# Norm in a four-layer block: per-column statistics once in a 128x512 bank per chunk, and a quarter of the high halves made by ScalarE

## The chip, the cores and the metric

One core of a Trainium2 chip runs the whole kernel. The metric is the device time of one execution in microseconds, as the median of several runs.

## The reference

The input x has 256 x 256 tokens of 64 channels, in fp32. Four layers of the same kind follow each other, each adding to x. Cut to what matters:

```python
xn = layernorm(x, norm_w, norm_b)              # over the 64 channels
left  = (xn @ Wl) * sigmoid(xn @ Wlg)          # some layers times a mask
right = (xn @ Wr) * sigmoid(xn @ Wrg)
og = sigmoid(xn @ Wog)
out = einsum('bikh,bjkh->bijh', left, right)   # or over k and the other side
out = layernorm(out, onorm_w, onorm_b) * og
x = x + out @ Wo
```

The change is in the first line: the normalisation of x in each layer.

## The kernel before, in words

Each layer is one block with a program per engine. The work is staged: `norm`, `project` (first half of the channels), a contraction, `project` (second half), a contraction, `finish`. The first two of them meet at the change: `norm` writes the normalised x to DRAM as two fp16 tensors, a high and a low part (XH or XHA), and `project` loads them again.

`norm` works on 16 chunks of 2048 columns by 128 partitions (two sides of 64 channels), a chunk being two tiles of 128x1024, so there are 32 tiles; tile t belongs to chunk t // 2. Per tile:

- `center` (TensorE, L663): eight 64x64 fp32 matmuls (four matmuls of two passes each) subtract the channel mean and scale by one number for the layer. The output is one of three two-bank PSUM buffers, `banks[t % 3]`. It waits until `scale` of tile t-3 has read that buffer, and for the first tile of a chunk until the chunk was loaded.
- `square` (ScalarE, L686), PSUM to SBUF.
- `vary` (TensorE, L670): two 128x128 matmuls with the constant K_MEAN make the mean of the squares over 64 channels, repeated on all 64 partitions of the side, in `banks[3]`.
- `root` (ScalarE, L692 and L696): logarithm, then exponential of -0.5 times it, both 128x1024.
- `scale` (VectorE, L712): the centred PSUM value plus a bias, times the result, to a ring of four SBUF tiles.
- `halve` (VectorE, L722 and L724): the high half as fp16, then what is left over as the low half. VectorE's order is scale(t), halve(t-1).

TensorE's order is center(0), center(1), and then vary(t), center(t+2) for each t. ScalarE's is square(t+1), root(t).

SyncE issues the transfers (L618, L626, L277, L298). The loads of x go to three chunk buffers; the load of chunk n+3 waits until both tiles of chunk n were centred. Its loop is, for each n:

```python
if n + 3 < from_dram:
    sp.wait_ge(centered.s, centered.n + 2 * n + 2)
    load_xt_chunk(sp, n + 3, n % 3)
if n >= 1:
    store(n - 1, (n - 1) % 2)   # waits for lows_ready of 2n tiles, then 4 DMAs
```

A load moves 1 MB, each of the four stores of a chunk 256 KB. In the first layer only eight chunks are loaded (`from_dram` is 8); the other eight stand in SBUF, and are stored to XT here, one DMA each. In the other layers all 16 are loaded, the first three outside this loop. At the end of the loop SyncE issues the first loads for `project`.

## Time and profile before

| | |
|---|---|
| median of 3 runs | 2152.81 us (2152.39 to 2152.84) |
| the profiled execution, its own time | 2150.95 us |
| its span, first to last instruction | 2148.8 us |
| mean granted TensorE clock | 0.956 |
| TensorE busy | 1888.1 us, 88% |
| VectorE busy | 1693.6 us, 79% |
| ScalarE busy | 1591.5 us, 74% |

The profile is of one execution. Durations in the next sections but one come from it; the time of an execution is 2.15 us more than its span. Busy shares are means over all stages. A line such as L663 is a line of the kernel's file. An instruction's duration contains the latency to its end, so that the next instruction of an engine can begin a little before it ends.

### The profile page before, as it was taken

The page shows a single profiled execution, that of the slowest core. Times are in us where ns is not written, and L with a number is a line of the kernel's source. Part 1 is how long each engine was busy: PE and PEld are TensorE (multiplying, and loading weights), DVE is VectorE, ACT ScalarE, POOL GpSimd, SP SyncE. Part 2 cuts the span into 40 slices and gives each one's busy share as a digit, 9 for nine tenths or more (in the row PEclk, how much of TensorE's full clock was granted, in tenths as well). Part 3 has the DMA queues.
Part 4 walks back from the last instruction along what each step waited for, and adds up shares of the span by engine and source line. Part 5 has one row for each costly group of instructions (what it writes and reads, how often), then busy time and mean ns, then how long its engine had stood idle before and what let it go on. Part 6 is the DMA issues. An engine that isn't in the chain of part 4 may idle for free. (4 is left out here: it accounts for less than half of the span.)

```text
span 2148.8 us, 44715 instructions
## 1 busy us (share of the span) xinstructions
PE 1888.1 (88%) x14485; PEld 1280.8 (60%) x14492; DVE 1693.6 (79%) x2690; ACT 1591.5 (74%) x2204; POOL 595.4 (28%) x574
## 2 busy tenths in 40 slices
PE   5687979699897998989989799899997879899998
PEld 4423959455422786855622697886552258777665
DVE  6798989989598877688969887878776977677665
ACT  3598969679897756569989775766888966566666
POOL 0001918175100000026400470732870000000755
PEclk8899989999999999999999999999999999999999
DMA  9589938279798739169979954917997993753897
GB/s 393 195 274 312 264 79 235 94 290 384 270 302 275 277 117 312 41 245 402 410 261 316 265 145 150 278 43 278 407 393 256 308 303 130 245 186 127 320 350 299
DMA packets 297397, 549.53 MB, mean 256 GB/s; under 512 B 14768, under 2 KB 170416, under 8 KB 273712
## 3 DMA queue, kind: packets, MB, share of 16 engines
q1 hardware_dynamic: 295680, 538.38, 72.9%
q10 hardware_dynamic: 1584, 9.51, 1.1%
q8 instruction: 68, 1.11, 0.2%
q14 instruction: 65, 0.53, 0.1%
HBM read 371.67 MB, written 176.16 MB: 255 GB/s over the span
## 5 line engine op out<-in xcount | busy, mean ns | idle before, releaser
L1603 POOL TENSOR_TENSOR LR<-LR 128x512 f32<-128x512 f32 x128 | 187.9, 1488 | 523.3 <-DVE LR L1649 501.2
L802 PE MATMUL bank<-whigh,kept 128*128 128x128 f16 x2048 | 268.2, 231 | 30.5 <-DMA kept<-XH 22.5
L1594 POOL TENSOR_TENSOR LR<-LR,sum 128x2048 f32<-128x2048 f32 x30 | 136.5, 4549 | 526.4 <-DVE LR L1408 526.4
L802 PEld LDWEIGHTS bank<-whigh,kept 128*128 128x128 f16 x2048 | 261.5, 150 | 34.6 <-issue 26.3
L802 PE MATMUL bank<-wlow,kept 128*128 128x128 f16 x2048 | 267.4, 230 | 0.0
L802 PEld LDWEIGHTS bank<-wlow,kept 128*128 128x128 f16 x2048 | 261.9, 150 | 0.0
L670 PE MATMUL bank<-LR,kst 128*128 128x512 f32 x512 | 254.3, 619 | 8.3 <-ACT LR L692 6.3
L865 POOL TENSOR_TENSOR msgs<-sigs,mask_sb 128x256 f32<-128x256 f32 x192 | 124.6, 663 | 487.1 <-ACT sigs L839 481.9
L1497 PEld LDWEIGHTS bank<-kst,LR 128*128 128x128 f32 x1024 | 151.0, 192 | 109.9 <-issue 90.7
L1509 PE MATMUL bank<-LR,wog 128*128 128x512 f16 x768 | 211.9, 385 | 4.8 <-ACT msgs L1550 4.0
L670 PEld LDWEIGHTS bank<-LR,kst 128*128 128x128 f32 x512 | 87.6, 191 | 179.1 <-issue 172.9
L812 PE MATMUL bank<-whigh,kept 128*128 128x128 f16 x2048 | 153.4, 226 | 37.1 <-DMA kept<-XHA 32.7
L1007 PE MATMUL bank<-LR 128*128 128x256 f32 x768 | 172.7, 387 | 7.0 <-DVE LR L904 4.2
L1263 PE MATMUL bank<-LR 128*128 128x256 f32 x768 | 169.9, 385 | 7.0 <-DVE LR L904 4.2
L1497 PE MATMUL bank<-kst,LR 128*128 128x128 f32 x1024 | 159.3, 279 | 14.7 <-ACT sigs L1545 7.7
L1007 PEld LDWEIGHTS bank<-LR 128*128 128x128 f32 x768 | 148.6, 194 | 28.3 <-DVE LR L904 4.6
L1263 PEld LDWEIGHTS bank<-LR 128*128 128x128 f32 x768 | 148.0, 193 | 28.2 <-DVE LR L904 4.6
L692 ACT ACTIVATE LR<-bank,epsx 128x1024 f32<-128x1024 f32 x128 | 142.9, 1116 | 25.7 <-PE bank L670 21.6
L812 PEld LDWEIGHTS bank<-whigh,kept 128*128 128x128 f16 x2048 | 121.1, 101 | 64.5 <-issue 36.3
L686 ACT ACTIVATE LR<-bank,small 128x1024 f32<-128x1024 f32 x128 | 140.8, 1100 | 16.5 <-PE bank L663 16.5
L839 ACT ACTIVATE sigs<-bank,small 128x256 f32<-128x256 f32 x256 | 121.1, 478 | 31.8 <-PE bank L802 25.4
L696 ACT ACTIVATE LR<-LR 128x1024 f32<-128x1024 f32 x128 | 135.5, 1058 | 4.0
(189 smaller groups left out, 4106.1 us busy)
## 6 DMA issues: line engine op xcount, KB each, us to landing
LR<-XT SPq DMA_DIRECT2D x103, 1024.0 KB, 8.9
kept<-XH SPq DMA_DIRECT2D x128, 512.0 KB, 5.8
kept<-XHA SPq DMA_DIRECT2D x128, 512.0 KB, 5.1
XT<-LR SPq DMA_DIRECT2D x56, 1024.0 KB, 9.0
LR<-XH SPq DMA_DIRECT2D x64, 512.0 KB, 6.7
LR<-XHA SPq DMA_DIRECT2D x64, 512.0 KB, 6.0
OS<-kept SPq DMA_DIRECT2D x12, 2048.0 KB, 7.5
LR<-OS SPq DMA_DIRECT2D x48, 512.0 KB, 8.5
```

Source lines behind the costliest of these rows:

```text
L670: last = pe.matmul(banks[3][:, u * BANK:(u + 1) * BANK], K(K_MEAN), sq[t % 3][:, u * BANK:(u + 1) * BANK], start=True, stop=True)
L686: act.activation(sq[t % 3], banks[t % 3][:, :], ACT.Square, bias=cb).then_inc(squared.s, 1)
L692: act.activation(lnv[t % 2], banks[3][:, :], ACT.Ln, bias=epsx[:, :], scale=1.0 / X_SCALE ** 2).then_inc(logged.s, 1)
L696: act.activation(rs[t % 3], lnv[t % 2], ACT.Exp, scale=-0.5).then_inc(rooted.s, 1)
L802: last = pe.matmul(bank(g)[:, j * P:(j + 1) * P], tokens(h, g // 4, g % 4, j, slice(0, P)), w[:, half * P:(half + 1) * P], start=part == 0 ...
L812: pe.matmul(bank(2 * q + s)[:, j * P:(j + 1) * P], tokens(h, s, q, j, slice(0, P)), whigh[:, half * P:(half + 1) * P], start=j == 0, stop= ...
L1007: last = pe.matmul(banks[e % 3][:, c * N:(c + 1) * N], src[:, kt, off_a + ch, ut * P:(ut + 1) * P], src[:, kt, off_b + ch, :], start=kt == ...
L1263: last = pe.matmul(banks[e % 3][:, c * N:(c + 1) * N], src[:, kt, off_a + 4 * g + c, ut * P:(ut + 1) * P], src[:, kt, off_b + 4 * g + c, : ...
L1497: last = pe.transpose(by_token(turn_bank(t))[:, :, j, :], n_t[c % len(nrm)][:, :, 4 * q + j], K(K_IDENT))
L1509: last = pe.matmul(bank(2 + t % 2), wog[w][:, :], pair_cols(x, q) if k_is_b else by_b(x, q), start=(w, part) == (0, 0), stop=w == 1)
L1594: pool.tensor_tensor(v, v, token(sum2, c, C), ALU.mult).then_inc(normalized.s, 1)
L1603: pool.tensor_tensor(by_b(x_of(c), q) if end else by_token_cols(x_of(c), q), by_token(gated[t % 4]), by_token_cols(xi[c % len(xi)], q), AL ...
```

## The change

The statistics are no longer made for each of the 64 partitions of a side, but once per column. `vary(n)` works on a chunk: four fp32 matmuls with 32 output columns (the constant K_STAT) put the variances of the chunk's four column blocks of 512 into four groups of 32 partitions of one 128x512 bank. There are two such banks in turn. Logarithm and exponential are made once per chunk on that bank. `spread_out(t)` is new: two fp32 matmuls over 32 rows each (K_SPREAD) carry a tile's values to all 128 partitions, into `banks[2]`.

`center` now alternates between `banks[0]` and `banks[1]`, and waits for the square of tile t-2 in place of `scale`. `take_out(t)` is new on ScalarE: it copies the centred tile, with the bias added, to one of six SBUF tiles. `scale` is a plain product of that tile and the spread values. In every fourth tile (3, 7, 11, ...) ScalarE makes the high half (`high_half`), and VectorE waits for it and makes the low half. The orders of TensorE and ScalarE are rewritten; those of VectorE and SyncE stay.

```diff
-K_CENTER, K_MEAN, K_GROUP, K_IDENT, K_DROP, K_LAST, K_SIDE, K_CENTER_OUT, K_END = \
-    0, 128, 256, 384, 512, 640, 768, 770, 898
+K_CENTER, K_SPREAD, K_GROUP, K_IDENT, K_DROP, K_LAST, K_SIDE, K_CENTER_OUT, K_STAT, K_END = \
+    0, 128, 256, 384, 512, 640, 768, 770, 898, 930
...
                          for v in (sum1, sum2))
-            sq, yc, lnv, rs = ([ar.take(GW) for _ in range(k)] for k in (3, 2, 2, 3))
+            sq, yc, xc = ([ar.take(GW) for _ in range(k)] for k in (1, 2, 6))
+            sq += [squares[0][:, :], squares[1][:, :], rings[0][0]]
             yc += [obuf[1][:, i * GW:(i + 1) * GW] for i in range(2)]
+            lnv, deviations = ([v[:, i * BANK:(i + 1) * BANK] for i in range(2)] for v in (ar.take(GW), rings[1][0]))
+            spread_rs, stat_bank = banks[2], [banks[3][:, i * BANK:(i + 1) * BANK] for i in range(2)]
             from_dram = FROM_DRAM if number == 0 else NCH
             cb, k_is_b = small[:, 7:8], layer["k_is_b"]
             per, tiles = 64, 2 * NCH
+            elsewhere = list(range(3, tiles, 4))
+            own = [t for t in range(tiles) if t not in elsewhere]
+
+            def parts_of(t):
+
+                h = t // 2 % 2
+                y, to, rest = (v.rearrange("p (s f) -> p s f", s=2) for v in (yc[t % 4], high[h], low[h]))
+                to, rest = (v[:, :, t % 2 * BANK:(t % 2 + 1) * BANK] for v in (to, rest))
+                return y, to, rest
+
             @block.sync
             def _(sp):
                 def store(n, h):
@@ -649,11 +667,11 @@
                     h = n % 3
                     if u == 0 and n < from_dram:
                         pe.wait_ge(loaded[h].s, loaded[h].n + 16 * (n // 3) + 16)
-                    pe.wait_ge(normed.s, normed.n + t - 2)
+                    pe.wait_ge(squared.s, squared.n + t - 1)
                     for half in range(2):
                         for s in range(2):
                             rows = slice(C * s, C * s + C)
-                            to = banks[t % 3][C * half:C * half + C, s * BANK:(s + 1) * BANK]
+                            to = banks[t % 2][C * half:C * half + C, s * BANK:(s + 1) * BANK]
                             x = xa[h] if n < from_dram else entered(n)
                             if k_is_b:
                                 cols = x[rows, (2 * half + u) * BANK:(2 * half + u + 1) * BANK]
...
@@ -663,64 +681,104 @@
                             last = pe.matmul(to, cen[rows, rows], cols, start=True, stop=True)
                     last.then_inc(centered.s, 1)
 
-                def vary(t):
-                    pe.wait_ge(squared.s, squared.n + t + 1)
-                    pe.wait_ge(logged.s, logged.n + t)
+                def vary(n):
+                    pe.wait_ge(squared.s, squared.n + 2 * n + 2)
+                    pe.wait_ge(logged.s, logged.n + n - 1)
                     for u in range(2):
-                        last = pe.matmul(banks[3][:, u * BANK:(u + 1) * BANK], K(K_MEAN),
-                                         sq[t % 3][:, u * BANK:(u + 1) * BANK], start=True, stop=True)
+                        for s in range(2):
+                            q = 2 * u + s
+                            last = pe.matmul(stat_bank[n % 2][32 * q:32 * q + 32, :], kst[:, K_STAT:K_STAT + 32],
+                                             sq[(2 * n + u) % 4][:, s * BANK:(s + 1) * BANK], start=True, stop=True)
                     last.then_inc(variance.s, 1)
 
-                center(0)
-                center(1)
-                for t in range(tiles):
-                    vary(t)
-                    if t + 2 < tiles:
-                        center(t + 2)
+                def spread_out(t):
+                    n, u = divmod(t, 2)
+                    pe.wait_ge(rooted.s, rooted.n + n + 1)
+                    pe.wait_ge(normed.s, normed.n + t)
+                    for s in range(2):
+                        rows = slice(32 * (2 * u + s), 32 * (2 * u + s) + 32)
+                        last = pe.matmul(spread_rs[:, s * BANK:(s + 1) * BANK], kst[rows, K_SPREAD:K_SPREAD + P],
+                                         deviations[n % 2][rows, :], start=True, stop=True)
+                    last.then_inc(spread.s, 1)
+
+                for t in range(3):
+                    center(t)
+                for n in range(NCH):
+                    vary(n)
+                    if n >= 1:
+                        spread_out(2 * n - 1)
+                    for t in (2 * n + 3, 2 * n + 4):
+                        if t < tiles:
+                            center(t)
+                    spread_out(2 * n)
+                spread_out(tiles - 1)
 
             @block.scalar
             def _(act):
+                def take_out(t):
+                    act.wait_ge(centered.s, centered.n + t + 1)
+                    act.wait_ge(normed.s, normed.n + t - 5)
+                    act.activation(xc[t % 6], banks[t % 2][:, :], ACT.Identity, bias=cb).then_inc(taken_out.s, 1)
+
                 def square(t):
-                    act.wait_ge(centered.s, centered.n + t + 1)
-                    act.wait_ge(variance.s, variance.n + t - 2)
-                    act.activation(sq[t % 3], banks[t % 3][:, :], ACT.Square, bias=cb).then_inc(squared.s, 1)
-
-                def root(t):
-
-                    act.wait_ge(variance.s, variance.n + t + 1)
-                    act.wait_ge(rooted.s, rooted.n + t - 1)
-                    act.activation(lnv[t % 2], banks[3][:, :], ACT.Ln, bias=epsx[:, :],
+                    act.wait_ge(variance.s, variance.n + t // 2 - 1)
+                    act.activation(sq[t % 4], banks[t % 2][:, :], ACT.Square, bias=cb).then_inc(squared.s, 1)
+
+                def logarithm(n):
+                    act.wait_ge(variance.s, variance.n + n + 1)
+                    act.wait_ge(rooted.s, rooted.n + n - 1)
+                    act.activation(lnv[n % 2], stat_bank[n % 2], ACT.Ln, bias=epsx[:, :],
                                    scale=1.0 / X_SCALE ** 2).then_inc(logged.s, 1)
-                    act.wait_ge(logged.s, logged.n + t + 1)
-                    act.wait_ge(normed.s, normed.n + t - 2)
-                    act.activation(rs[t % 3], lnv[t % 2], ACT.Exp, scale=-0.5).then_inc(rooted.s, 1)
-
+
+                def root(n):
+                    act.wait_ge(logged.s, logged.n + n + 1)
+                    act.wait_ge(spread.s, spread.n + 2 * n - 2)
+                    act.activation(deviations[n % 2], lnv[n % 2], ACT.Exp, scale=-0.5).then_inc(rooted.s, 1)
+
+                def high_half(t):
+                    y, to, _ = parts_of(t)
+                    act.wait_ge(normed.s, normed.n + t + 1)
+                    act.wait_ge(stored[t // 2 % 2].s, stored[t // 2 % 2].n + per * (t // 4))
+                    act.activation(to, y, ACT.Identity, bias=scale1[:, :]).then_inc(odd_highs.s, 1)
                 for h in range(4):
                     act.wait_ge(stored[h].s, stored[h].n)
-                square(0)
-                for t in range(tiles):
-                    if t + 1 < tiles:
-                        square(t + 1)
-                    root(t)
+                for t in range(2):
+                    take_out(t)
+                    square(t)
+                for n in range(NCH):
+                    if n + 1 < NCH:
+                        take_out(2 * n + 2)
+                        square(2 * n + 2)
+                    logarithm(n)
+                    if n + 1 < NCH:
+                        take_out(2 * n + 3)
+                    root(n)
+                    if 2 * n - 1 in elsewhere:
+                        high_half(2 * n - 1)
+                    if n + 1 < NCH:
+                        square(2 * n + 3)
+                high_half(tiles - 1)
 
             @block.vector
             def _(dve):
                 def scale(t):
 
-                    dve.wait_ge(rooted.s, rooted.n + t + 1)
+                    dve.wait_ge(spread.s, spread.n + t + 1)
+                    dve.wait_ge(taken_out.s, taken_out.n + t + 1)
                     dve.wait_ge(lows_ready.s, lows_ready.n + t - 3)
-                    dve.scalar_tensor_tensor(yc[t % 4], banks[t % 3][:, :], cb, rs[t % 3], ALU.add, ALU.mult).then_inc(normed.s, 1)
+                    dve.tensor_tensor(yc[t % 4], spread_rs[:, :], xc[t % 6], ALU.mult).then_inc(normed.s, 1)
 
                 def halve(t):
 
-                    h = t // 2 % 2
-                    y, to, rest = (v.rearrange("p (s f) -> p s f", s=2) for v in (yc[t % 4], high[h], low[h]))
-                    to, rest = (v[:, :, t % 2 * BANK:(t % 2 + 1) * BANK] for v in (to, rest))
+                    y, to, rest = parts_of(t)
                     dve.wait_ge(normed.s, normed.n + t + 1)
                     if t % 2 == 0:
-                        dve.wait_ge(stored[h].s, stored[h].n + per * (t // 4))
-                    dve.tensor_scalar(to, y, X_SCALE, None, ALU.add).then_inc(highs_ready.s, 1)
-                    dve.wait_ge(highs_ready.s, highs_ready.n + t + 1)
+                        dve.wait_ge(stored[t // 2 % 2].s, stored[t // 2 % 2].n + per * (t // 4))
+                    if t in elsewhere:
+                        dve.wait_ge(odd_highs.s, odd_highs.n + elsewhere.index(t) + 1)
+                    else:
+                        dve.tensor_scalar(to, y, X_SCALE, None, ALU.add).then_inc(highs_ready.s, 1)
+                        dve.wait_ge(highs_ready.s, highs_ready.n + own.index(t) + 1)
                     dve.scalar_tensor_tensor(rest, y, X_SCALE, to, ALU.add, ALU.subtract).then_inc(lows_ready.s, 1)
 
                 for h in range(4):
...
     k[:, K_CENTER:K_CENTER + P] = np.eye(P) - same_side / C
     k[:, K_CENTER_OUT:K_CENTER_OUT + P] = np.eye(P) - same_side / C
-    k[:, K_MEAN:K_MEAN + P] = same_side / C
+    k[:, K_SPREAD:K_SPREAD + P] = (np.arange(P)[:, None] % 32 == 0) & (np.arange(P)[None, :] < C)
+    k[:, K_SPREAD:K_SPREAD + P] += (np.arange(P)[:, None] % 32 == 16) & (np.arange(P)[None, :] >= C)
```

## Rows read from the trace of the kernel before

**Rows 1.** The page, part 1: busy us (share of the span) and instructions

```profile
PE 1888.1 (88%) x14485; PEld 1280.8 (60%) x14492; DVE 1693.6 (79%) x2690; ACT 1591.5 (74%) x2204; POOL 595.4 (28%) x574
```

**Rows 2.** Stretches: us, busy time of each engine, TensorE clock, DMA share, GB/s

```profile
640.00:650.00 10.00, 9.18 (x40) 2.69 (x36) 9.45 (x10) 9.37 (x10) 0.00 (x0) 1.00 0.93 311
```

**Rows 3.** Timeline, first layer's norm: start, us, engine, line

```profile
139.99 1.28 DVE L712 SCALAR_TENSOR_TENSOR LR<-bank,small,LR 128x1024 f32<-128x1024 f32 x1 [0.28 <-ACT LR L696]
...
141.32 1.09 PE L663 MATMUL bank<-LR,cen 64*64 64x512 f32 x8 [0.36 <-DVE LR L712]
...
142.15 1.06 ACT L696 ACTIVATE LR<-LR 128x1024 f32<-128x1024 f32 x1
...
142.34 1.98 PE L670 MATMUL bank<-LR,kst 128*128 128x512 f32 x4
...
143.11 1.10 ACT L686 ACTIVATE LR<-bank,small 128x1024 f32<-128x1024 f32 x1
...
144.36 1.11 ACT L692 ACTIVATE LR<-bank,epsx 128x1024 f32<-128x1024 f32 x1 [0.15 <-PE bank L670]
...
146.60 1.28 DVE L712 SCALAR_TENSOR_TENSOR kept<-bank,small,LR 128x1024 f32<-128x1024 f32 x1 [0.22 <-ACT LR L696]
...
147.80 0.68 DVE L722 TENSOR_SCALAR sum<-kept 128x1024 f16<-128x1024 f32 x1
```

**Rows 4.** Groups by line and form: busy, mean ns, idle before

```profile
L1641 DVE SCALAR_TENSOR_TENSOR LR<-bank,prm,LR 128x512 f32<-128x512 f32 x128 | 95.1, 744 | 16.7 <-PE bank L1516 15.0 <-DMA LR<-XT 1.1
...
L1634 DVE TENSOR_TENSOR sigs<-bank,msgs 128x512 f32<-128x512 f32 x64 | 43.8, 685 | 1.8 <-issue 1.8
...
L1021 ACT ACTIVATE kept<-bank 128x1024 f32<-128x1024 f32 x48 | 49.2, 1025 | 92.6 <-PE bank L1007 86.9 <-DVE sum L1056 5.7
...
L1381 ACT ACTIVATE sum<-sum,epso 128x256 f32<-128x256 f32 x8 | 4.0, 504 | 1.2 <-DVE sum L1374 1.2
...
L1383 ACT ACTIVATE sum<-sum 128x256 f32<-128x256 f32 x8 | 3.3, 418 | 0.3
```

**Rows 5.** Lines 663 and 812, second layer: ns min/median/max, first and last start

```profile
L663 PE MATMUL bank<-LR,cen x176: 589/611/1112, 571.7 to 676.3; 64*64 64x512 f32 x176
...
L812 PE MATMUL bank<-whigh,kept x62: 219/314/314, 687.0 to 699.9; 128*128 128x128 f16 x62
```

**Rows 6.** Timeline of SyncE's queue and its neighbours, second layer's norm

```profile
602.59 1.23 DVE L724 SCALAR_TENSOR_TENSOR LR<-LR 128x1024 f16<-128x1024 f32 x1
...
603.90 3.41 SPq L277 DMA_DIRECT2D XHA<-LR  x4
...
607.36 1.10 SPq L298 DMA_DIRECT2D LR<-XT  x1
...
618.97 1.09 PE L663 MATMUL bank<-LR,cen 64*64 64x512 f32 x8 [0.46 <-DVE kept L712]
```

**Rows 7.** Loads (L298): load 5, loads 6 to 15; first layer's 3 to 7

```profile
DMA to landing us min/median/max: 7.4/7.4/7.4
...
DMA to landing us min/median/max: 7.3/8.4/8.9
...
DMA to landing us min/median/max: 4.7/7.6/8.7
```

**Rows 8.** Timeline, end of the first layer's norm

```profile
192.81 3.04 SPq L277 DMA_DIRECT2D XH<-sum  x4
...
195.95 2.12 SPq L303 DMA_DIRECT2D kept<-XH  x2
...
202.86 0.33 PE L802 MATMUL bank<-whigh,kept 128*128 128x128 f16 x1 [5.69 <-DMA kept<-XH]
```

**Rows 9.** Waits on TensorE at 1212:1222, and the stretch behind

```profile
PE bank L802 <- DVE LR L893: 2.1, 1, 2.1
...
1215.70:1219.10 3.40, 3.40 (x35) 3.40 (x34) 1.24 (x4) 1.91 (x4) 1.23 (x2) 0.50 1.17 290
```

**Rows 10.** Timeline, the first two tiles' centring in the second layer

```profile
571.75 3.69 PE L663 MATMUL bank<-LR,cen 64*64 64x512 f32 x16 [0.71 <-PEq L545]
```

More of the change, by code:

```diff
@@ L170, in build @@
         epsx = sb("epsx", [P, 1])
+        scale1 = sb("scale1", [P, 1])
         banks = [ctx.enter_context(nc.psum_tensor(f"bank{i}", [P, GW], F32)) for i in range(4)]
@@ L190, in build @@
         centered = sem("centered")
+        taken_out = sem("taken_out")
         variance = sem("variance")
+        spread = sem("spread")
         squared = sem("squared")
@@ L196, in build @@
         highs_ready = sem("highs_ready")
+        odd_highs = sem("odd_highs")
         lows_ready = sem("lows_ready")
@@ L446, in _ @@
                 dve.memset(epsx[:, :], EPS / X_SCALE ** 2)
+                dve.memset(scale1[:, :], X_SCALE)
         fold_project, fold_turn, fold_spread, fold_act, fold_start, fold_copy, fold_greatest, fold_row, fold_rest = fold(0)
@@ L733, in norm @@
             advance(*((loaded[h], 16 * len(range(h, from_dram, 3))) for h in range(3)), (stored[2], 16 * (NCH - from_dram)), (stored[0], per * NCH // 2), (stored[1], per * NCH // 2),
-                    (centered, 2 * NCH), (variance, 2 * NCH), (squared, 2 * NCH), (logged, 2 * NCH),
-                    (rooted, 2 * NCH), (normed, 2 * NCH), (highs_ready, 2 * NCH),
+                    (centered, 2 * NCH), (taken_out, 2 * NCH), (squared, 2 * NCH), (variance, NCH), (logged, NCH),
+                    (rooted, NCH), (spread, 2 * NCH), (normed, 2 * NCH), (highs_ready, len(own)),
+                    (odd_highs, len(elsewhere)),
                     (lows_ready, 2 * NCH))
@@ L1697, in constants @@
     k[:, K_CENTER_OUT:K_CENTER_OUT + P] = np.eye(P) - same_side / C
-    k[:, K_MEAN:K_MEAN + P] = same_side / C
+    k[:, K_SPREAD:K_SPREAD + P] = (np.arange(P)[:, None] % 32 == 0) & (np.arange(P)[None, :] < C)
+    k[:, K_SPREAD:K_SPREAD + P] += (np.arange(P)[:, None] % 32 == 16) & (np.arange(P)[None, :] >= C)
+    k[:, K_STAT:K_STAT + 32] = (np.arange(P)[:, None] // C == np.arange(32)[None, :] // 16) / C
     k[:, K_GROUP:K_GROUP + P] = (pair_of[:, None] == pair_of[None, :]) / 4
```

## The prediction, made before the change was run

> **What bounds the kernel now.** I read the page first: TensorE is busy for 88% of the span, VectorE 79%, ScalarE 74% [rows 1]. That is an average over stages, and the change touches one of them, the norm, which runs four times. So the second view was the table of stretches inside a norm. The reader is to see there that three engines and the DMA engines are all at 92 to 95% [rows 2]. Busy shares don't say which one decides. The timeline does [rows 3]. Follow one tile's chain: `scale` (L712, starts 139.99, 1.28 us) ends; `center` starts 0.05 us behind it (141.32); TensorE, in order, starts `vary` 1.02 us later (142.34, 1.98 us); logarithm 144.36, an exponential of 1.06 behind it, next but one `scale` 146.60 to 147.88. From end of `scale` to end of `scale`: 147.88 - 141.27 = 6.61 us for two tiles, one chunk. It is a loop of latencies, not a full engine: ScalarE's next square starts at 143.11, 0.96 us after an exponential of 1.06 us began (142.15), so instructions that don't wait for each other overlap by 0.10 us, and the pitch of a free 128x1024 one is 1.00 us. A norm takes 687.0 - 571.7 = 115.3 us from its first `center` to the first matmul of `project` [rows 5].
>
> The third view is the DMA queue's own [rows 6, 7]. SyncE issues in program order: the four stores of chunk c-5, then the load of chunk c. In the second layer's norm, `halve` of tile 5 ends at 602.59 + 1.23 = 603.8; the stores are issued from 603.90 for 3.41 us (3.04 in [rows 8], where less else is under way), load 7 at 607.36; loads take 8.4 us to land (7.3 to 8.9), so it is there at about 615.8, and `center` of tile 14, which reads it, starts at 618.97. Slack: 3 us. No wait shows it, and the change spends it.
>
> **The change, part by part.** Hops, all from [rows 3]: 0.05 us into TensorE, 0.04 from it, 0.03 between ScalarE and VectorE. Tiles are numbered from 0, chunk n has tiles 2n and 2n+1, R(n) is the end of `root(n)`.
>
> *ScalarE.* Removed: a 128x1024 logarithm and exponential per tile (1.12 and 1.06 us). Added: one 128x512 pair per chunk, one `take_out` per tile, a `high_half` every fourth tile. `take_out` has the shape and bias operand of the square: 1.10 us; its lower bound is the plain copy of that shape, 1.025 [rows 4]; I take 1.10. Exponential of 512 columns: 256 take 0.418 and 1024 take 1.058, so 0.63. Logarithm: 256 take 0.504, 1024 take 1.116, so 0.70 [rows 3, 4]. `high_half`: 1.06 to 1.10. Sum of pitches per chunk: 4 x 1.00 + 0.60 + 0.53 + 0.50 = 5.6 us, under today's 6.6.
>
> *VectorE.* `scale` becomes a product of a PSUM and an SBUF operand: 0.685 us at 512 columns [rows 4] and the 0.53 us that the next 512 cost in this engine's fp32 forms (1.28 against 0.74) give 1.22 us. A high half takes 0.68, a low half 1.23 [rows 3, 6]. `halve` starts 0.08 before `scale` ends; less such overlaps it is 5.6 us per chunk. Not the bound.
>
> *TensorE.* `center` stays: four quadrants at once, all eight fp32 passes in 1.09 us [rows 3]. The 32-row `spread_out` and 32-column `vary` are not in the trace. If their groups run at once like the quadrants, which differ in rows and in columns, a block takes 1.09 us with the next starting 1.02 later; if one after another, `spread_out` (two matmuls of two passes) takes `vary`'s 1.98 us and the new `vary` (four) about 3.7. I take 1.09, as the quadrants are the nearest row; the other end is a rival. The Trainium skill, TensorEngine Tiling (Array Packing), Tiling Modes, says that a change of tiling mode drains the engine, and the new order changes mode four times per chunk, which speaks against it. The row on `center` then `vary` is such a change and costs 1.02 to the next start: already in my blocks. A full drain, 1.09 each, would add some 2 us to the whole.
>
> *The loop without any transfer.* Chunk with a `high_half` (every other): R, high half (pitch 1.0), square ends R+2.0; `vary` +0.05, `spread_out` +1.02, `center` +1.02, its end +1.13, `take_out` pitch 1.0, `root` 0.63: 6.85 us. Other chunks: `spread_out(2n)` 0.05+1.09, `scale` 0.05+1.22, `spread_out(2n+1)` 0.05+1.02, `center` 1.13, `take_out` 1.0, `root` 0.63: 6.25. Mean 6.55 against 6.61: nothing is won by the halved work, because the chain got two matmul blocks. The head: R(0) about 10.5 us behind the first `center` (1.9 us for each of the first two at the low clock [rows 10]). R(12) = 10.5 + 5 x 6.85 + 7 x 6.27 = 88.6, and `center(30)`, behind square and three blocks, 5.1 later: 93.7. The tail: after `center(30)` come three blocks, `take_out(31)`, `root(14)`, `spread_out(28)`, `scale(28)`, the halves of 27, the stores of chunk 13 (3.1 us) and the first load of `project`, 6.9 us (issue 195.95, first matmul 202.86 [rows 8]): 20.8 us. 114.5 us, against 115.3.
>
> *The loads, where the cost is.* Today `center` of tile 2c waits for `scale(2c-3)`; the low halves that release the stores of chunk c-5 follow `scale(2c-8)`: five tiles between, 15 us. After it, `center(2c)` waits only for squares and for its place behind `spread_out(2c-5)`, which needs `scale(2c-6)`: two tiles. Worked out: halves of 2c-9 end at R+3.6 or R+4.3, `center(2c)` is ready at R+11.3, so 7.0 to 7.7 us are left, and the queue needs 3.1 to 3.4 of issuing and the landing. With idle transfers ahead of the stores, load 5 took 7.4 us behind the first stores (issue 593.74) [rows 7]. 10.5 is over 7.7, for every load from chunk 5 on. Then a new loop closes, two chunks long: load(c) lands, `center(2c)` 0.97 to the next start, `spread_out(2c-4)` queued behind it 1.09, hop and pitch of `scale` 1.18, high half 0.72 (not where ScalarE made it), low half 1.23, SyncE's hop and four issues 3.25, load(c+2) lands 7.3, hop 0.05: 15.8 us (15.1 without the high half; the slower of the two interleaved loops leads). TensorE idles some 3 us in each. A gap of 2.1 us was followed by half clock for 3.4 us elsewhere [rows 9], and a `center` takes 1.85 instead of 1.09 then; as that will not happen each time, I add 0.5: 16.3.
>
> `center(10)` can start when load 5 is there: R(1) is 16.7, the halves of tile 1 end 4.3 later at 21.0, issues 3.1 [rows 8], landing 7.3: 31.5. `center(30)`: 31.5 + 5 x 16.3 = 113.0 instead of 93.7, so 19.3 late, and a norm is 19.3 - 0.8 = 18.5 us longer. Three layers: 55.5. The first layer loads eight chunks only, the rest stands in SBUF, and its loads land up to 8.7 us late [rows 7]: `center(10)` at 32.8, `center(14)` 17.6 later at 50.4, against 10.5 + 3 x 6.27 + 6.85 + 5.1 = 41.3: 9.1, less 0.8: 8.3. Sum: +63.8 us. The profiled execution took 2150.95 us (span 2148.8 and 2.15 around it): 2214.8; the median of the runs stands 1.86 above it: **2216 us**. The constants, the one memset, the new semaphores lie in the first 90 us beside loads: nothing. `project` and later stages move, unchanged.
>
> **The rivals.** *The loads come in time.* For it: 4.7 us is the shortest landing [rows 7]. It decides at 2 x 6.55 - 8.5 = 4.6 us. Against it: that was without stores ahead, and these always stand ahead. Then each norm is 0.8 shorter and the sum is 2150, or about 2136 if `take_out`, blocks and hops are also each at their lower ends (0.25 less per chunk, 56 chunks): the case on the other side.
> *The groups don't run at once.* If `spread_out` takes 1.98, the load loop grows by 0.9: 15 x 0.9 = 14, 2230. If `vary` takes 3.7 too, the chain of the squares is the longer: 6.55 + 2.6 + 0.9, some 3.4 us over today's for 56 chunks, 2340.
> *The clock falls in each idle stretch and stays low for the blocks behind it.* `center` and `spread_out` cost 0.8 each more, 1.6 per loop instead of 0.5: 16 x 1.1 = 18, 2234. For it, the 2.1 us gap; against it, gaps of 0.3 to 0.4 us in every tile cost nothing today [rows 3].
>
> **How the numbers follow.** Forecast 0.74; loads in time 0.13; groups in turn 0.06; low clock 0.07. Around the forecast, landings of 6.5 to 8.5 us (16 loops x 0.8 down, 1.2 up) and issuing of 3.0 to 3.4 give 2200 to 2240. The range 2180 to 2245 adds partly smaller stalls below and the clock above; outside are most of the first rival and a slow `vary`. Within 0.2% (4 us, about what a measurement of this kernel can tell from no change) lies part of the first rival: faster 0.08, same 0.04, slower 0.88.
>
> **What would show it.** `center` (the new line of its matmul) waiting for the DMA of `xt` in every chunk from 5 on, 2 to 4 us; pairs of chunks 16 us apart; loads landing in 7 to 8 us; ScalarE and VectorE waiting for TensorE; DMA share in a norm falling from 0.93 to under 0.8; `take_out` at 1.10, `spread_out` and `vary` blocks at 1.09. A norm of some 134 us where the layer loads all chunks, 124 in the first. I am wrong if `center` never waits for a load, if a load behind four stores lands in under 5 us, or if a later stage takes back the delay.

## The result

The changed kernel took **2268.9 us** (median of 4 runs, 2262.1 to 2274.8), the kernel before, on the same chip, 2152.6 (4 runs): a ratio of 1.054 [1.051, 1.058]. It is slower, by 116 us where 63.8 were forecast. The direction and the place were right, the size was not, and the time lies outside the range (2180 to 2245).

The page of the profile after, against [rows 1]: all three engines are idle for longer, and TensorE's clock is lower.

```profile
span 2269.4 us, 45750 instructions
PE 1948.0 (86%) x15004; PEld 1264.1 (56%) x15004; DVE 1662.8 (73%) x2659; ACT 1553.3 (68%) x2236; POOL 594.5 (26%) x574
PEclk8887989999876899989977699999997769999999
L721 ACT ACTIVATE LR<-bank,small 128x1024 f32<-128x1024 f32 x128 | 142.7, 1115 | 144.5 <-PE bank L681 140.0
L769 DVE TENSOR_TENSOR LR<-bank,LR 128x1024 f32<-128x1024 f32 x64 | 78.4, 1225 | 135.2 <-PE bank L700 135.2
L681 PE MATMUL bank<-LR,cen 64*64 64x512 f32 x752 | 135.2, 824 | 25.3 <-DMA LR<-XT 18.7
```

L681 is `center`, L690 `vary`, L700 `spread_out`, L721 `take_out`, L725 `square`, L730 and L736 logarithm and exponential, L742 `high_half`, L769 `scale`, L780 and L782 the halves. The three dips of the clock row (slices 11 to 13, 21 to 23, 31 to 33) are the norms of the last three layers. ScalarE now waits 140 us for TensorE in `take_out`, and VectorE 135 us in the `scale` group shown and 79 us in its twin with the other output name. TensorE itself waits 36 us for loads in `center` (18.7 in the group shown, 17.2 in its twin). So the load wait alone can't be all of it: TensorE must also be slow in between.

The stretch of [rows 2], then the second layer's whole norm, in windows of after (columns as in [rows 2]):

```profile
640.00:650.00 10.00, 9.03 (x44) 2.09 (x36) 6.67 (x8) 6.72 (x9) 0.00 (x0) 0.72 0.78 236
592.00:738.60 146.60, 116.64 (x512) 25.58 (x512) 89.05 (x86) 92.45 (x104) 0.00 (x0) 0.73 0.66 209
```

VectorE and ScalarE fell from 95 and 94% to 67%, the DMA share from 0.93 to 0.78, the clock from 1.00 to 0.72. From the first `center` to the first matmul of `project` the four norms took 114.9, 115.3, 116.0 and 115.3 us before, and 131.2, 146.6, 148.4 and 145.5 after: 110.2 us of the span's 120.6. The other 10 lie outside the norms, where the code is the same: 1687.3 us before and 1697.6 after. The profiles of the experiments below that leave that code as it is have 1682.1 to 1696.4 us there. Why it varies was not looked into. The 10 us are not put down to the change.

The timeline of after, second layer (start, us, engine, line):

```profile
641.05 2.08 PE L700 MATMUL bank<-msgs,kst 32*128 32x512 f32 x4
641.72 3.31 SPq L281 DMA_DIRECT2D XHA<-sum  x4
643.06 3.19 PE L681 MATMUL bank<-LR,cen 64*64 64x512 f32 x16
645.08 0.89 SPq L302 DMA_DIRECT2D kept<-XT  x1
...
646.80 1.13 PE L700 MATMUL bank<-msgs,kst 32*128 32x512 f32 x4 [0.55 <-ACT msgs L736]
647.85 0.62 PE L690 MATMUL bank<-LR,kst 128*32 128x512 f32 x2
...
648.31 0.60 PE L690 MATMUL bank<-LR,kst 128*32 128x512 f32 x2
...
650.40 1.09 PE L681 MATMUL bank<-LR,cen 64*64 64x512 f32 x8
651.94 1.09 PE L681 MATMUL bank<-kept,cen 64*64 64x512 f32 x8 [0.45 <-DMA kept<-XT]
...
654.16 0.83 SPq L302 DMA_DIRECT2D LR<-XT  x1
656.28 1.13 PE L700 MATMUL bank<-msgs,kst 32*128 32x512 f32 x4
657.34 1.09 PE L681 MATMUL bank<-kept,cen 64*64 64x512 f32 x8
...
662.20 1.57 PE L681 MATMUL bank<-LR,cen 64*64 64x512 f32 x8 [3.78 <-DMA LR<-XT]
663.70 2.08 PE L700 MATMUL bank<-msgs,kst 32*128 32x512 f32 x4
665.71 1.07 PE L690 MATMUL bank<-LR,kst 128*32 128x512 f32 x2
```

Two things are to be seen. Four stores are issued, the load directly behind them at 645.08, and `center` waits for it till 651.94, 6.9 us later; the next load, 654.16, is waited for till 662.20, 8.0 us: the load loop as forecast. And each block exists in two sizes. `spread_out` takes 1.13 or 2.08, `center` 1.09 or some 1.6 to 2.0, a half of `vary` 0.62 or 1.07. These are the two clock levels, 2.4 and 1.2 GHz. Behind the wait of 3.78 us the clock is at its lower level.

It also falls where no load is awaited. In the first layer nothing is loaded from chunk 8 on, and the matmuls and windows of after show there:

```profile
159.34 1.13 PE L700 MATMUL bank<-msgs,kst 32*128 32x512 f32 x4 [0.89 <-ACT msgs L736]
161.38 1.07 PE L690 MATMUL bank<-squares,kst 128*32 128x512 f32 x2 [0.91 <-ACT sigs L725]
...
163.24 2.08 PE L700 MATMUL bank<-msgs,kst 32*128 32x512 f32 x4
165.25 3.16 PE L681 MATMUL bank<-LR,cen 64*64 64x512 f32 x16
```

```profile
137.00:160.90 23.90, 18.35 (x116) 4.37 (x108) 20.64 (x21) 20.09 (x24) 0.00 (x0) 1.00 0.69 205
160.90:167.70 6.80, 6.32 (x24) 1.50 (x28) 4.27 (x5) 3.52 (x5) 0.00 (x0) 0.50 0.94 322
```

TensorE had worked 18.35 of 23.9 us and stood idle 0.89 and 0.91 us at a time; then come 6.8 us at half clock. A chunk with such a stretch in it takes 9.6 us, against 6.45 or 6.9 at the full clock. So does one that lies in low clock from end to end, as this one of the second layer (`center(12)` to `center(14)`):

```profile
635.20:644.80 9.60, 9.55 (x36) 1.98 (x32) 5.35 (x6) 6.37 (x7) 0.00 (x0) 0.50 0.73 235
```

TensorE works 9.55 of these 9.60 us. At the lower level it is TensorE, and no wait, that sets the pace. The Trainium skill, TensorE: Matmul & The Clock Gate, A second HAM failure mode, tells of a kernel in which short idle spells between groups of matmuls made the clock swing between its levels; the rows above, with idle spells of 0.89 and 0.91 us, agree.

Two causes are thus on the table, and each may bring the other about: late loads, and a clock that falls because the chain leaves TensorE idle. The experiments separate them.

### The profile page after: what moved, and what is told of

It is laid out like the page before. It is cut to its first block and busy times, and to the rows that moved or that the text cites. A ratio compares the mean times of both kernels' runs of the same rounds, so it can differ in the third digit from the quotient of the medians.

```text
span 2269.4 us, 45750 instructions
## 1 busy us (share of the span) xinstructions
PE 1948.0 (86%) x15004; PEld 1264.1 (56%) x15004; DVE 1662.8 (73%) x2659; ACT 1553.3 (68%) x2236; POOL 594.5 (26%) x574
## 5 line engine op out<-in xcount | busy, mean ns | idle before, releaser
L924 POOL TENSOR_TENSOR msgs<-sigs,mask_sb 128x256 f32<-128x256 f32 x192 | 124.6, 664 | 542.1 <-ACT sigs L898 536.2
L721 ACT ACTIVATE LR<-bank,small 128x1024 f32<-128x1024 f32 x128 | 142.7, 1115 | 144.5 <-PE bank L681 140.0
L700 PE MATMUL bank<-msgs,kst 32*128 32x512 f32 x512 | 192.0, 833 | 54.0 <-ACT msgs L736 31.7
L871 PE MATMUL bank<-whigh,kept 128*128 128x128 f16 x2048 | 155.1, 228 | 31.3 <-DMA kept<-XHA 23.9
L769 DVE TENSOR_TENSOR LR<-bank,LR 128x1024 f32<-128x1024 f32 x64 | 78.4, 1225 | 135.2 <-PE bank L700 135.2
L700 PEld LDWEIGHTS bank<-msgs,kst 32*128 32x128 f32 x512 | 49.6, 232 | 207.1 <-issue 120.9
L681 PE MATMUL bank<-LR,cen 64*64 64x512 f32 x752 | 135.2, 824 | 25.3 <-DMA LR<-XT 18.7
```

What stands on the lines that cost most here:

```text
L681: last = pe.matmul(to, cen[rows, rows], cols, start=True, stop=True)
L700: last = pe.matmul(spread_rs[:, s * BANK:(s + 1) * BANK], kst[rows, K_SPREAD:K_SPREAD + P], deviations[n % 2][rows, :], start=True, stop=True)
L721: act.activation(xc[t % 6], banks[t % 2][:, :], ACT.Identity, bias=cb).then_inc(taken_out.s, 1)
L871: pe.matmul(bank(2 * q + s)[:, j * P:(j + 1) * P], tokens(h, s, q, j, slice(0, P)), whigh[:, half * P:(half + 1) * P], start=j == 0, stop= ...
L924: pool.tensor_tensor(msg[g], sig[g], mask_sb[:, kt, bass.ds(m, 4)].unsqueeze(1).broadcast_to([P, C, 4]), ALU.mult).then_inc(gates_masked.s, 1)
```

## The experiments

Each was timed beside the kernel before on the same chip; a ratio is to it, with its 95% interval. The kernel before had medians of 2155.0 us beside the first four, 2152.6 beside the wait filled by 3.0 us, the two with the centring first and the control, and 2153.3 beside the others. A "norm" is the stretch from the first `center` to the first matmul of `project`, from the timeline; the length of a chunk is the time from `center(2n)` to `center(2n+2)`. Each edit moves the line numbers, so a line is named by what it does where one is shown.

**Loads ahead of the stores.** SyncE issues the load of chunk c before the four stores of chunk c-5:

```diff
-                    if n + 3 < from_dram:
-                        sp.wait_ge(centered.s, centered.n + 2 * n + 2)
-                        load_xt_chunk(sp, n + 3, n % 3)
+                    for c in ((3, 4) if n == 0 else (n + 4,)):
+                        if c < from_dram:
+                            sp.wait_ge(centered.s, centered.n + 2 * (c - 3) + 2)
+                            load_xt_chunk(sp, c, c % 3)
```

> The changed kernel, with the load of chunk c issued before the stores of chunk c-5 instead of behind them; nothing else. Load theory alone (late loads cause the loss, and the low clock only follows their waits): no wait of the centring for a load behind chunk 5, 6.5 to 6.7 us per chunk, norms of about 117 us, 2155 to 2165 us. Clock theory (the clock falls by itself because the new order leaves TensorE idle for 0.9 us several times per chunk, and the late loads only add to it): norms of about 127 us, as the first layer's last seven chunks took 7.46 us each in the changed kernel without any load; granted clock in the norms between 0.6 and 0.9; about 2200 us.

2190.3 us, 1.017 [1.015, 1.020]: 79 us less than after. No `center` waits for a load any more. The norms take 124.6, 127.1, 120.7 and 118.5 us; TensorE is at the low clock for 36, 38, 22 and 16 us of them, after 49, 78, 80 and 81 in the changed kernel. A late load is the larger cause, and it brings low clock with it; low clock without it remains. It does not come in each norm: the window below, 87 us of the fourth norm, has the same idle spells, 0.89 us in every chunk and 0.91 us in every second one, with TensorE busy for 77%, and the clock holds.

```profile
1664.00:1751.00 87.00, 66.61 (x420) 16.66 (x416) 70.62 (x68) 74.22 (x85) 0.00 (x0) 1.00 0.84 279
```

What decides whether it falls is not settled by any run here.

**Fill against the low clock.** Small fp16 matmuls whose result nobody reads go into a PSUM bank that is overwritten next; `fill(n, 4)` takes 1.04 us.

```diff
+                def fill(n, times):
+                    if n + 1 < NCH:
+                        pe.wait_ge(logged.s, logged.n + n)
+                        for _ in range(times):
+                            pe.matmul(stat_bank[(n + 1) % 2], ident_fill, moving_fill, start=True, stop=True)
...
+                    fill(n, 4)
                     spread_out(2 * n)
+                    if 2 * n - 1 in elsewhere:
+                        fill(n, 4)
```

> The changed kernel with its late loads, and four fp16 128x128x512 matmuls (about 0.86 us) on constants in two idle stretches of TensorE: ahead of spread_out(2n), and behind it in the chunks with a high half; they write the statistics bank that the next vary overwrites. If the low clock is a cause of its own: clock near 1.0 in the norms, a loop of 15.8 to 16.5 us per two chunks from the late loads, 2205 to 2225 us. If the clock matters little, the fill only costs time: 2270 us or more.

2262.5 us, 1.050 [1.047, 1.053]. A miss. In the first layer's chunks without loads it did what it was to do (6.45 and 6.9 us each, no low clock), but elsewhere the fill stands inside the load loop, ahead of the `spread_out` on which the next stores hang, and lengthens it by 0.97 us. This run says nothing against the clock, and nothing for it in the loaded chunks.

**Both.** The loads early and the fill.

> Both edits: loads earlier and TensorE filled. If the two causes together are the whole loss: 6.5 to 6.9 us per chunk, norms of 115 to 120 us, clock near 1.0, 2150 to 2170 us. If a third cause is there (the extra matmul blocks in the chain cost more than I worked out), it stays above 2175 us with neither a load wait nor a low clock.

2165.8 us, 1.006 [1.004, 1.008]. The windows of the second layer's norm, with loads early and with both (that of after is above):

```profile
583.20:710.30 127.10, 98.21 (x512) 23.43 (x513) 88.79 (x86) 91.58 (x104) 0.00 (x0) 0.85 0.74 241
```
```profile
580.00:698.10 118.10, 107.32 (x601) 28.21 (x601) 89.56 (x87) 92.16 (x104) 0.00 (x0) 0.93 0.79 260
```

The clock goes from 0.73 over 0.85 to 0.93, the norm from 146.6 over 127.1 to 118.1. The chunks now take 6.94 and 6.45 us in turn, 6.70 in the mean. So some 24.5 us of the 116 are low clock that comes without any late load, and the difference to the kernel before is down to 13 us.

**All high halves on VectorE**, nothing else changed: `elsewhere = []`, and the last `high_half` dropped.

> The changed kernel with every high half on VectorE again (the second half of the change undone). Load theory: the loop through the late loads holds the low half and, in every tile now, the high half: 15.8 us or more per two chunks as before, and the ScalarE chain gets shorter by 1.0 us in every other chunk, which only counts where no load is late: 2255 to 2270 us. If ScalarE's part of the chain is what costs: at least 20 us less, under 2250 us.

2255.7 us, 1.048 [1.045, 1.050], 13 us less than after. 7.5 of them are in the first norm: its chunks without loads take 6.45 us each, and the clock stays up. The windows of that stretch in after, and in this run:

```profile
130.00:190.00 60.00, 50.24 (x268) 11.74 (x260) 45.73 (x45) 46.60 (x53) 0.00 (x0) 0.86 0.75 244
```
```profile
130.00:190.00 60.00, 48.32 (x298) 12.09 (x292) 54.39 (x55) 48.70 (x57) 0.00 (x0) 0.98 0.84 275
```

The idle spell of 0.9 us ahead of `spread_out` is still there in every chunk. The one of 0.91 us ahead of `vary` (161.38 above), where the square stands behind ScalarE's high half, is gone. So here the clock holds without that second spell. This is one norm only, and with the loads early the clock held for 87 us with both spells, so that it is their doing is not shown. In the loaded layers the norms still take 148.1, 146.1 and 143.7 us: ScalarE's high half is a small part of what the change costs. Whether moving it would also end the low clock once the loads come early was not run without the fill.

**The wait filled.** To see the load loop at the full clock, `fill(n, 14)`, 3.0 us, stands ahead of the `center` that waits for the load.

```diff
+                        if t == 2 * n + 4 and 5 <= n + 2 < from_dram:
+                            fill(n, 14)
                         if t < tiles:
                             center(t)
                     spread_out(2 * n)
+                    if 2 * n - 1 in elsewhere:
+                        fill(n, 4)
```

> The changed kernel with its late loads, but TensorE is kept busy while it waits for one: fourteen fp16 matmuls on constants (3.0 us at the high clock) between the centring of tile 2n+3 and that of 2n+4 in the chunks whose load comes late, and four behind spread_out in the chunks with a high half. The fill of the run before this one stood inside the loop of the late loads (behind the centring) and lengthened it by 0.97 us; this one stands where TensorE idles anyway. Two causes, loads and low clock: the waits for loads shrink but the loop stays, now with all blocks at the high clock, 15.8 to 16.6 us per two chunks, norms of 132 to 137 us, 2205 to 2225 us. If the loop itself was mis-worked and the clock is not what makes it 18.1 us: 2255 us or more.

2262.0 us, 1.051 [1.048, 1.055]. A miss, and nothing is decided by it: low clock is down to 11 to 20 us per norm, but each chunk's own chain runs through the 3.0 us (8.8 and 9.25 us per chunk in turn), and from `center(12)` on no `center` waits for a load. The fill became the bound.

**The wait filled by less.** `fill(n, 6)` takes 1.47 us in the same place. `fill(n, 4)` stands ahead of `spread_out(2n)` where no load is awaited, and behind it in every other chunk.

> The changed kernel, its loads still late. TensorE gets six fp16 matmuls whose results nobody reads (1.3 us) ahead of the centring of every loaded even tile from chunk 5 on, where it waits for a transfer, and four (0.9 us) ahead of the block that spreads an even tile where no load is awaited, and behind that block every other chunk. The earlier fill of 3.0 us stood in the chain of the chunk itself; 1.3 us is less than the wait it stands in. Theory (the load loop costs 15.8 us per two chunks, and what came on top of it is low clock): a granted clock of at least 0.95 in the norms, 15.8 to 16.4 us per two chunks, norms of the later layers of 131 to 136 us, 2205 to 2225 us. Rival (the load loop itself is longer than predicted, since landings take over 8 us once the stores follow closely): 17.5 us or more per two chunks at a high clock, 2240 us or more. If the clock still falls with idle stretches of under 1.5 us, neither is told apart.

2234.7 us, 1.036 [1.034, 1.039]. The time is 10 us above the expected one, for a reason that the norms show: 124.7, 134.7, 142.0 and 133.3 us. In the third, from `center(14)` on, TensorE waited up to 2.8 us for a load, the clock still fell, and a chunk there takes up to 11.4 us. One such wait:

```profile
1173.92 1.87 PE L681 MATMUL bank<-LR,cen 64*64 64x512 f32 x8 [1.93 <-DMA LR<-XT]
1175.72 2.08 PE L700 MATMUL bank<-msgs,kst 32*128 32x512 f32 x4
```

In the fourth the clock stayed up between `center(10)` and `center(30)`. The window of that stretch, and issues and matmuls of its timeline (L710 is the fill):

```profile
1717.00:1797.00 80.00, 71.44 (x404) 18.64 (x408) 57.08 (x55) 58.48 (x65) 0.00 (x0) 1.00 0.82 264
```
```profile
1745.32 3.36 SPq L281 DMA_DIRECT2D XHA<-sum  x4
1748.73 0.88 SPq L302 DMA_DIRECT2D LR<-XT  x1
```
```profile
1745.78 1.09 PE L681 MATMUL bank<-kept,cen 64*64 64x512 f32 x8
1746.80 1.47 PE L710 MATMUL bank<-kst 128*128 128x512 f16 x6
1749.16 1.09 PE L681 MATMUL bank<-LR,cen 64*64 64x512 f32 x8 [0.89 <-DMA LR<-XT]
1750.18 1.13 PE L700 MATMUL bank<-msgs,kst 32*128 32x512 f32 x4
```

The blocks are at their full-clock times on both sides of the load wait. `center(10)` starts 33.5 us and `center(30)` 112.8 us behind the first `center`: 79.3 us for five turns, **15.9 us per two chunks**; the second layer has 80.8, so 16.2, one chunk at the low clock among them. The prediction's clean loop was 15.8. The loads land in 7.3 to 7.9 us here.

**The order of the blocks.** The changed chain ends a chunk with `center(2n+3)` behind `vary` and `spread_out`. Here it stands ahead of both, with the loads early:

```diff
                 for n in range(NCH):
+                    if 2 * n + 3 < tiles:
+                        center(2 * n + 3)
                     vary(n)
                     if n >= 1:
                         spread_out(2 * n - 1)
-                    for t in (2 * n + 3, 2 * n + 4):
-                        if t < tiles:
-                            center(t)
+                    if 2 * n + 4 < tiles:
+                        center(2 * n + 4)
                     spread_out(2 * n)
```

> Loads earlier, and TensorE's order changed: centre(2n+3), vary(n), spread_out(2n-1), centre(2n+4), spread_out(2n), so that two matmul blocks less stand between a square and the next take_out. The loop theory: ScalarE's pitch of 5.6 us and the transfers (2 MB per chunk, 6.2 us at their share of 0.93 in 6.7) are the bounds, 6.2 to 6.4 us per chunk; with the clock falling now and then 2135 to 2165 us. If the order of the blocks is not what makes 6.7 us per chunk: 2185 to 2195 us as with the loads alone.

2172.6 us, 1.008 [1.005, 1.011]: 18 us less than loads early alone by the times, 21 by the ratios (1.017). Low clock is still some 35 us per norm. Where the clock is up, the chunks take 5.62 and 7.02 us in turn, 6.32 in the mean, as the loop theory had it.

> As the run before, with four fp16 matmuls on constants ahead of spread_out(2n) and four behind it in the chunks with a high half, to keep the clock. Loop theory: 6.2 to 6.4 us per chunk in all norms, center(30) at 88 to 92 us, 2130 to 2145 us, faster than the kernel before. If fill and real blocks get in each other's way: 2150 to 2165 us.

With the fill 2161.0 us, 1.004 [1.002, 1.006] (10 runs): a miss, since 2130 to 2145 was expected. The chunks take 6.1 and 7.1 us in turn, 6.6 in the mean: the fill that holds the clock costs some 0.3 us per chunk. `center(30)` starts 95.2 us into a norm, in the mean of four, where the kernel before needs 100.2. Yet the norms take 117.2 against 115.4: the lead is lost behind `center(30)`. Matmuls at the end of the second layer's norm (L701 is `spread_out`, L782 `scale`, L884 `project`):

```profile
679.57 1.13 PE L701 MATMUL bank<-msgs,kst 32*128 32x512 f32 x4
682.11 1.13 PE L701 MATMUL bank<-msgs,kst 32*128 32x512 f32 x4 [1.42 <-DVE LR L782]
685.44 2.08 PE L701 MATMUL bank<-msgs,kst 32*128 32x512 f32 x4 [2.20 <-DVE kept L782]
690.25 1.88 PE L884 MATMUL bank<-whigh,kept 128*128 128x128 f16 x16 [2.74 <-DMA kept<-XHA]
```

The last tiles' values are spread one by one, each behind the `scale` of the tile before, which in VectorE's order stands behind halves, and `project` waits for its first load, which is issued behind four stores.

**The kernel before with its loads early**, as a control for the first edit:

> The kernel before the change, with the loads issued earlier in the same way. Its loads had 3 us of slack, so the load theory expects no difference: within 0.3% of the kernel before. If the transfers held the norm in a way that no wait shows, at least 4 us less.

2168.9 us, 1.008 [1.005, 1.010]: a miss, it is slower. The waits of its norm (600 to 690 us; L298 is the load, L664 `center`, L723 the high half) show why:

```profile
SPq L298 <- PE bank L664: 21.4, 10, 3.2
DVE LR L723 <- DMA XHA<-LR: 5.1, 4, 1.7
DVE sum L723 <- DMA XHA<-sum: 4.3, 4, 1.9
```

Here centring comes late in the chunk, so SyncE waits for `centered`, which it does not in the same stretch of the kernel before, and holds back stores that are ready. VectorE then waits for the buffers that they read. Of these two kernels, the early load pays in the changed one alone.

**The high halves on VectorE, with all three edits**:

> Loads before the stores, centring first, four small matmuls as fill, and all high halves on VectorE. Theory (the chunk is a chain through ScalarE and three TensorE blocks, and the high half on ScalarE lengthens it by 1.0 us in every other chunk): against the same kernel with ScalarE's high halves (6.62 us per chunk) the chunks with a high half fall from 7.05 to about 6.1, so some 6.2 us each, norms of 110 to 113 us, 2130 to 2145 us. Rival (VectorE becomes the bound: its 1.22, 0.68 and 1.23 us per tile less overlaps are 5.9 us per chunk, and its waits add to that): 6.5 us or more per chunk, 2155 us or more.

2158.7 us, 1.002 [1.001, 1.003], with the next one the fastest of the changed norms, but it misses the expected time; the rival's time, 2155 us or more, has it. Some chunks take 6.1 us as expected, others 6.5 to 7.0, where VectorE waits for stores to end (600 to 690 us; L792 is the high half):

```profile
DVE LR L792 <- DMA XHA<-LR: 4.1, 5, 1.9
DVE sum L792 <- DMA XHA<-sum: 1.8, 4, 0.8
```

**The first load for `project` ahead of the stores of chunk 13.** The same edit on the centre-first kernel with fill, and on the kernel before:

```diff
+                    if n == NCH - 2:
+                        for h in range(2):
+                            sp.wait_ge(stored[h].s, stored[h].n + per * (4 if k_is_b else 5))
+                        load_xh_chunk(sp, 0, 0, k_is_b)
                     if n >= 1:
                         store(n - 1, (n - 1) % 2)
...
-                for h in range(2):
-                    sp.wait_ge(stored[h].s, stored[h].n + per * (4 if k_is_b else 5))
-
-                load_xh_chunk(sp, 0, 0, k_is_b)
```

> Loads before the stores, centring first and fill, as tried before (2161 us, norms of 117 us), and the first load for the next stage issued before the stores of chunk 13 instead of behind them. Theory (the longer end of a norm is partly the wait for that load: TensorE idles 2.7 us for it): norms 2.3 to 2.9 us shorter, 114.5 us, 2149 to 2153 us. Rival (the next stage's ScalarE or VectorE work, or its second load, is late anyway): the first matmul of the next stage comes earlier, but the time stays at 2158 to 2162 us.

> The kernel before, with the first load for the next stage issued before the stores of chunk 13 and nothing else changed. TensorE waited 5.7 us for that load at the end of the first layer's norm. Theory: each norm ends 3 to 5 us earlier and the time falls by 12 to 18 us, to 2135 to 2141 us. Rival (the stage behind catches up, because its later loads and ScalarE set its pace): within 4 us of the kernel before.

2158.1 us, 1.0025 [1.001, 1.004], and 2150.6 us, 0.998 [0.9973, 0.9996]. Both times are the rivals'. The norms are shorter, 461.1 us in sum against 468.8 and 456.6 against 461.6, but the medians fall by 2.9 and 2.7 us only. That the stages behind take back the rest is likely, not shown: what lies outside the norms differs by more than that from profile to profile. The kernel before with this edit is at the edge of what a measurement can tell, and nothing that was tried beats the kernel before clearly.

## Why the prediction failed

**What held.** The place: `center` waits for the load in the loaded chunks, and the loop load, `center`, `spread_out`, `scale`, halves, four issues, load takes 15.9 us at the full clock, in the fourth norm of the short fill (15.8 worked out). The groups run at once: `spread_out` 1.13, `vary` 0.62 and 0.60 one behind the other, 1.06 in all, `center` 1.09. A block behind another of a different shape starts 1.05 us after it (647.85 - 646.80), 0.08 before its end. The Trainium skill, TensorEngine Tiling (Array Packing), Tiling Modes, has the engine drained at such a change. What the rows of the run with both edits show of it is small (L682 is `center`, L711 the fill):

```profile
675.90 1.09 PE L682 MATMUL bank<-kept,cen 64*64 64x512 f32 x8
676.81 1.04 PE L682 MATMUL bank<-LR,cen 64*64 64x512 f32 x8
...
682.35 1.09 PE L682 MATMUL bank<-LR,cen 64*64 64x512 f32 x8
683.37 1.04 PE L711 MATMUL bank<-kst 128*128 128x512 f16 x4
```

Behind a `center` another one starts after 0.91 us, a block of another shape after 1.02: 0.11 us more, which the prediction's 1.02 had in it. The estimated durations: `take_out` 1.115 for 1.10, logarithm 0.70, exponential 0.62 for 0.63, `scale` 1.225 for 1.22, `high_half` 1.14 for 1.06 to 1.10. The chain without transfers: 6.70 per chunk at the full clock for 6.55. The tail, from `center(30)` to `project`: 22.3 us in the second layer for 20.8, part of it at the low clock. The last addition was a little off (2214.8 and 1.86 make 2216.7).

**What failed** is one term, the price of the clock in the loop: "as that will not happen each time, I add 0.5: 16.3". The loop took (124.3 - 33.6)/5 = 18.1 us per two chunks in the second layer. With 33.6 for 31.5 at `center(10)` and the tail, the norm of 146.6 is accounted for: 5 x 1.8 + 2.1 + 1.5 = 12.6 of the 12.8 us over the forecast 133.8. The clock did fall nearly each time, TensorE being at its lower level for 78 of 146.6 us. And the term was of the wrong kind. It priced a slower `center` in a loop still set by the load. But at the low clock a chunk needs 9.6 us by itself, 19.2 for two, which is above the load loop's 15.8. The forecast wait "in every chunk from 5 on" was there in five, six and five of the eleven such chunks of the later three layers, and lasted 0.2 to 4.3 us; the others were not waiting for a load at all. The same error stands in "the loop without any transfer", where full clock was taken for granted: the first layer's last seven chunks took 7.46 us each, not 6.55, and made 6 of the 8 us by which that norm was mis-forecast.

**The rival** of the falling clock had 0.07 and 2234 us. It named what happened, again as a surcharge and with too small a price (2.3 us per turn measured, 1.6 given). It was set aside because gaps of 0.3 to 0.4 us cost nothing before; the change made them 0.9 us. The change's narrower blocks also do a chunk's statistics in some 3.2 us of TensorE's time (one `vary`, two `spread_out`) where two `vary` blocks took 4.0, and the high half on ScalarE adds an idle spell ahead of `vary` in every other chunk. To leave TensorE idle was an effect of the change itself, not only of the load; how often the clock falls for it differs from norm to norm.

**The sum by runs.** From 2268.9, the short fill takes 34 us (low clock, with the fills' own cost in it). From there to both edits it is 69 us (2234.7 to 2165.8). These are mostly the load loop, but not it alone: the fills stand in other places in the two runs, and the short fill still has 12 to 33 us of low clock per norm. By the other path, loads first, it is 79 and 24.5: the causes overlap by some 10 us, since the waits bring low clock. Without the 0.5 for the clock, the forecast's load loop comes to some 56 of its 63.8 us.

The last 13 us do not lie in the chain. From `center(10)` to `center(30)` a norm with both edits takes 66.9 us, and the kernel before 67.1 in the layers that load all chunks, where its chunks take 6.71 us, and 66.4 in the first. (The 6.61 us that the prediction took for today's chunk is from chunks without loads.) Over the four norms `center(10)` comes 13.7 us earlier in sum, and the stretches from `center(30)` to `project` are 27.3 us longer in sum, 21.3 to 23.3 us each against 14.4 to 16.3. Why the waits in the third norm of the short fill were longer than in the fourth (1.93 against 0.89 us), and the clock fell in the one and held in the other, is not settled: no run varied that alone.

## What to carry to other kernels

When a change takes work off TensorE in a chain of latencies, price the whole stage at the lower clock as well, as a rival loop and not as a surcharge on the awaited instruction: whichever loop is longer at the clock that will be granted sets the pace. A transfer queue served in program order has a slack per transfer that no wait shows; it should be worked out before a change moves its producer or its consumer. Where a stage became shorter, look at its last tiles: here 5 us won in the loop were lost behind the last chunk, and of a quicker end only a part reached the total.

## What the runs showed of the hardware

The granted clock fell to 0.50 for 6.8 us in a stretch where TensorE had been busy 77% (18.35 of 23.9 us) and idle for no longer than 0.92 us at a time. It held at 1.00 for 87 us in another run with the same idle spells and the same busy share (66.61 of 87 us). These rows do not tell what decides. At 0.50 a chunk took 9.6 us, with TensorE busy for 9.55 of them, for 6.45 or 6.9 at the full clock. 1.0 us of fp16 matmuls that nobody reads, once or twice a chunk, brought the second layer's norm from a clock of 0.85 to 0.93 and 25 us off the kernel. fp32 matmuls of 32 rows by 128 columns in two row groups, and of 128 rows by 32 columns in four column groups, ran side by side: two of the first took 1.13 us and four of the second 1.06 us, where two full-size ones, one behind the other, took 1.98. In the second layer's norm of after, a 1 MB load landed 4.7 to 4.8 us after its issue with nothing ahead of it, and 6.6 to 8.0 us after it behind four stores of 256 KB; over all layers of the kernel before it took up to 9.3 us behind them.
